# Half-height projections and one bank for the turned scores in a four-head expert attention

## What is computed

```python
sx = einsum('bsh,ndh->bnsd', x, hl_w) + hl_b        # 4 heads n, d = 16
q = einsum('bnsd,neod->bneso', sx, wq)              # 4 expert queries e per head
k = einsum('bnsd,nod->bnso', sx, wk)
v = einsum('bnsd,nod->bnso', sx, wv)
scores = einsum('bnesd,bntd->bnest', q, k) * d ** 0.5 + causal
att = softmax(scores, axis=-1)
qkv = einsum('bnest,bntd->bnesd', att, v)
# then a gate over e, the mix, two layer norms and a small feed-forward network
```

## Time and profile before

| | |
|---|---|
| median of 3 runs | 2512.23 us (2507.62 to 2513.51) |
| profiled execution | 2496.42 us |
| its span | 2494.4 us |
| TensorE busy over the span | 77% |
| VectorE busy over the span | 69% |
| ScalarE busy over the span | 37% |

### The profile page before, as it was taken

How to read it: one execution, slowest core, us unless ns; L and a number is a source line. 1 busy time by engine, 2 the same in 40 slices (tenths; PEclk the granted TensorE clock), 3 DMA queues, 4 the chain that set the end, 5 groups by cost and what they waited for, 6 DMA issues and landing times. The chain is left out here.

```text
span 2494.4 us, 51482 instructions
## 1 busy us (share of the span) xinstructions
PE 1922.1 (77%) x15831; PEld 1495.5 (60%) x15831; DVE 1715.0 (69%) x5200; ACT 919.3 (37%) x2958; POOL 1029.3 (41%) x878
## 2 busy tenths in 40 slices
PE   6888888799999999999999626777533332999970
PEld 2367767677777777777777414556422221887860
DVE  0069888358888888888888659999588883333223
ACT  2354343234444444444444238888422210111100
POOL 0023332013434434434443322222168875777772
PEclk9966676589999999999999656777755555555555
DMA  9900000000000000000000000000000002655526
GB/s 297 320 10 0 0 0 0 1 2 2 2 1 0 0 0 0 0 0 0 0 0 0 1 0 1 1 1 0 1 19 23 22 23 83 183 165 150 156 85 160
DMA packets 119880, 106.65 MB, mean 43 GB/s; under 512 B 62448, under 2 KB 109680, under 8 KB 118896
## 3 DMA queue, kind: packets, MB, share of 16 engines
q1 hardware_dynamic: 87024, 73.88, 11.0%
q10 hardware_dynamic: 18432, 16.79, 2.3%
q0 software_dynamic: 14336, 14.91, 1.8%
HBM read 78.84 MB, written 26.67 MB: 42 GB/s over the span
## 5 line engine op out<-in xcount | busy, mean ns | idle before, releaser
L988 ACT ACTIVATE arena<-PS 128x384 f32<-128x384 f32 (+3 forms) x384 | 178.3, 482 | 562.2 <-DMA arena<-in_t_experts_dram 216.5
L1336 POOL DMA_INDIRECT expert_rows<-arena x256 | 246.9, 965 | 104.4 <-issue 77.6
L1494 DVE TENSOR_REDUCE XR<-PS 128x2 f32<-128x192 f32 (+2 forms) x768 | 173.7, 280 | 107.4 <-PE PS L642 107.2
L642 PE MATMUL PS<-arena 32*128 32x96 f32 (+2 forms) x3072 | 235.0, 286 | 0.0
L1323 POOL DMA_INDIRECT routed_rows<-XR,SLu x192 | 199.8, 1041 | 74.9 <-issue 68.2
L642 PEld LDWEIGHTS PS<-arena 32*128 32x128 f32 x3072 | 199.1, 193 | 20.7
L1024 ACT ACTIVATE XR<-PS 128x256 f32<-128x256 f32 x512 | 167.3, 381 | 67.2 <-PE PS L657 67.0
L1277 POOL TENSOR_TENSOR arena<-arena,mhalf 96x16 f32<-96x16 f32 x32 | 92.7, 2896 | 225.8 <-DVE arena L1540 225.8
L1498 DVE TENSOR_TENSOR XR<-PS,XR 128x192 f32<-128x192 f32 (+2 forms) x768 | 172.4, 278 | 0.0
L609 PE MATMUL PS<-arena,WP 128*128 128x192 f32 x640 | 152.1, 363 | 18.4 <-ACT arena L988 17.8
L657 PE MATMUL PS<-WP,XR 128*128 128x128 f32 (+1 forms) x1024 | 163.7, 284 | 1.0 <-ACT XR L1024 1.0
(11 more groups left out here) (304 smaller groups left out, 4716.9 us busy)
## 6 DMA issues: line engine op xcount, KB each, us to landing
arena<-in_x_dram SPq DMA_DIRECT2D x32, 784.0 KB, 9.2
arena<-in_t_experts_dram ACTq DMA_DIRECT2D x128, 128.0 KB
arena<-in_t_experts_dram SPq DMA_DIRECT2D x128, 128.0 KB
routed_rows<-zt SPq DMA_DIRECT2D x16, 528.0 KB, 6.2
arena<-routed_rows SPq DMA_DIRECT2D x64, 132.0 KB
expert_rows<-arena POOLq DMA_INDIRECT x256
WP<-in_t_pack_dram SPq DMA_DIRECT2D x1, 3425.0 KB, 19.4
routed_rows<-XR,SLu POOLq DMA_INDIRECT x192, 2.2
```

The lines of the kernel that those rows point to most:

```text
L642: mm = pe.matmul(PS[:, i, S_AT[j]:S_AT[j] + QB * (j + 1)], qF[rows, u, 3 * b + j, :], kF[rows, u, keys], start=False, stop=True, skip_grou ...
L988: return act.activation(dst, src, ACT.Identity, **kw)
L1336: pool.indirect_dma_start(YD, bass.IndirectOffsetOnAxis(yi[:, u % 4, k:k + 1], 0), yb[:, u % 4, k, :], None).then_inc(e_st[u % 2], 16)
L1494: dve.tensor_reduce(negmax[:, p, j, :], PS[:, 0:2, S_AT[j]:S_AT[j] + QB * (j + 1)], AX_X, ALU.max, negate=True).then_inc(b_max, 1)
```

## The change

Keys and queries: each of the two matmuls of `project` takes only the 64 rows in which its images lie, and writes a bank of its own (`Q_` and `Q_ + 1`, now banks 2 and 3). The result comes out ordered by row half and not by image, so the consumers read it at `at = 2 * (b % 2) + b // 2`, and ScalarE's copies read two banks of 192 columns in one instruction. Turned scores: both heads of a turn go into one bank (`T0_`, now bank 6), ScalarE takes the exponential of 512 columns in one instruction, and `b_exp` counts once per turn. The transposes of the next turn wait for the whole exponential of the last one.

```diff
-            T0_, O_, F_, Q_, Z_ = 2, 4, 5, 6, 7
+            Q_, O_, F_, T0_, Z_ = 2, 4, 5, 6, 7
...
-                    o = PS[:, bk, 0:G * NTOK].rearrange("p (q r t) -> p q r t", q=2, r=2)[:, :, par, :]
-                    mm = pe.matmul(o, w[:, par, :], sxF[:, u, :].rearrange("p (q t) -> p q t", q=2),
+                    mm = pe.matmul(PS[:, Q_ + par, 0:FC], w[halves(par), par, :], sxF[halves(par), u, :],
                                    start=True, stop=True)
...
+                    at = 2 * (b % 2) + b // 2
...
-                        keys = slice(b * NTOK, b * NTOK + QB * (j + 1))
+                        keys = slice(at * NTOK, at * NTOK + QB * (j + 1))
...
-                            if n == 0:
-                                wait(pe, b_exp, 2 * k - 1 + i)
-                            mm = pe.transpose(PS[0:keys, T0_ + i, n * P:(n + 1) * P], Pe[:, p, i, n * P:n * P + keys], ident[:, :])
+                            if n == 0 and i == 0:
+                                wait(pe, b_exp, k)
+                            mm = pe.transpose(PS[0:keys, T0_, (2 * i + n) * P:(2 * i + n + 1) * P], Pe[:, p, i, n * P:n * P + keys], ident[:, :])
...
-                    pe.wait_ge(b_exp, (g * G + b) * 4 + 4)
+                    pe.wait_ge(b_exp, (g * G + b) * 2 + 2)
...
-                act.activation(kF[:, u, :], bank(Q_, P, G * NTOK), ACT.Identity,
+                act.activation(kF[:, u, :].rearrange("p (r n) -> p r n", r=2), PS[:, Q_:Q_ + 2, 0:FC], ACT.Identity,
...
-                    for i in range(2):
-                        act.wait_ge(b_pt, ((g * G + b) * 2 + p) * 2 + i + 1)
-                        act.activation(PT[:, b % 2, 2 * p + i, :], bank(T0_ + i, P, 2 * P), ACT.Exp).then_inc(b_exp, 1)
+                    act.wait_ge(b_pt, ((g * G + b) * 2 + p) * 2 + 2)
+                    act.activation(PT[:, b % 2, 2 * p:2 * p + 2, :].rearrange("p h n -> p (h n)"), bank(T0_, P, 4 * P),
+                                   ACT.Exp).then_inc(b_exp, 1)
```

More of the change, by code:

```diff
@@ L603, in b_values, with project @@
                 to_tokens(sxF[:, u, :], F_, GC).then_inc(b_vs, 1)
-            def project(w, u, bk):
+            def project(w, u):
                 for par in range(2):
-                    o = PS[:, bk, 0:G * NTOK].rearrange("p (q r t) -> p q r t", q=2, r=2)[:, :, par, :]
-                    mm = pe.matmul(o, w[:, par, :], sxF[:, u, :].rearrange("p (q t) -> p q t", q=2),
+                    mm = pe.matmul(PS[:, Q_ + par, 0:FC], w[halves(par), par, :], sxF[halves(par), u, :],
                                    start=True, stop=True)
@@ L615, in b_keys @@
                 wait(pe, b_gd, g - 2)
-                project(f_wk, u, Q_).then_inc(b_k, 1)
+                project(f_wk, u).then_inc(b_k, 1)
             def b_query(e):
@@ L621, in stage @@
                     wait(pe, b_qk, g * NE + e)
-                    project(f_wq[:, :, e, :], u, Q_).then_inc(b_q, 1)
+                    project(f_wq[:, :, e, :], u).then_inc(b_q, 1)
                 return stage
@@ L638, in stage @@
                     for j in BANDS:
-                        keys = slice(b * NTOK, b * NTOK + QB * (j + 1))
+                        keys = slice(at * NTOK, at * NTOK + QB * (j + 1))
                         for i in range(2):
                             rows = slice(32 * (2 * p + i), 32 * (2 * p + i) + 32)
-                            mm = pe.matmul(PS[:, i, S_AT[j]:S_AT[j] + QB * (j + 1)], qF[rows, u, 3 * b + j, :],
+                            mm = pe.matmul(PS[:, i, S_AT[j]:S_AT[j] + QB * (j + 1)], qF[rows, u, 3 * at + j, :],
                                            kF[rows, u, keys], start=False, stop=True, skip_group_check=True)
@@ L1013, in stage @@
                     wait(act, b_s, (g - 1) * 2 * G)
-                    copy_out(qF[:, u, :, e * QB:(e + 1) * QB],
-                             bank(Q_, P, G * NTOK).rearrange("p (m t) -> p m t", t=QB)).then_inc(b_qk, 1)
+                    copy_out(qF[:, u, :, e * QB:(e + 1) * QB].rearrange("p (r m) t -> p r m t", r=2),
+                             PS[:, Q_:Q_ + 2, 0:FC].rearrange("p r (m t) -> p r m t", t=QB)).then_inc(b_qk, 1)
                 return stage
@@ L1439, in _ @@
             dve.wait_ge(a_h, NG)
-            dve.memset(PS[64:P, 2:4, P:2 * P], 0.0).then_inc(b_clear, 1)
-            O_, F_, Q_, Z_ = 4, 5, 6, 7
+            dve.memset(PS[64:P, 6, :].rearrange("p (i n c) -> p i n c", i=2, n=2)[:, :, 1, :], 0.0).then_inc(b_clear, 1)
+            Q_, O_, F_, Z_ = 2, 4, 5, 7
             def groups_of(t, n):
```

## The result

The changed kernel is slower: median 2614.65 us (2611.74 to 2630.39) against 2509.93 us for the kernel before in the same comparison, ratio 1.043, 95% interval 1.039 to 1.048. The profiled execution has a span of 2609.8 us against 2494.4, 115 us more. Forecast were 2500 us and a chance of 0.08 for slower.

The account below looks back on a forecast made before the run. A ring of waits between engines, not TensorE alone, bounds the attention stage; 10.5 us from two projections plus 2 us at the start, 12.5 together, take 2512.2 to 2500 us, range 2486 to 2511 us.

Parts of the forecast that it names:

- The ring: Attention turn's cycle of waits between engines, 28.85 us; only `b_query(1)` and `b_query(2)` of five projections lie on it.
- the 10.5 of the sum: Attention stage: two projections on the cycle save 0.35 us a turn, over 30 turns at full clock 10.5 us.
- The 2 us for the first groups: First two groups, at 0.70 of full clock: TensorE sets the pace with all five projections, estimated 2 us saved.
- The cost of a projection: One `project` call on TensorE, start to start: 0.75 us before, 0.52 us at 64 rows.
- step costs: TensorE changing tile height: stepping out priced at 0.09 us, slower start of the piece behind at 0.06 us.
- Keys, `b_query(0)` and `b_query(3)` "at nothing": These three projections gain nothing in steady turns, because VectorE's chain covers them; without that cover, 0.34 us a turn.
- The rival: Granted clock falls around the grown idle time before `b_query(1)`; 2527 us with one turn at the lower level; chance 0.07.
- the growth to 0.9 us: TensorE's wait before `b_query(1)` grows from 0.53 to about 0.9 us as keys and `b_query(0)` shrink.
- Its price of 27 us: A whole attention turn at the 1.2 GHz level would last some 27 us longer.
- The chain behind 1016.05 "as long as now": VectorE's stretch from 1016.05 until L1513 ends at 1029.30, busy without a sizeable wait, keeps its length.
- The turned scores and the two-bank copies: Single 512-column exponential and ScalarE's copies from two banks: taken as no gain and no cost.

Follow-up runs that it names:

- b4: Changed kernel with keys and first query projection at 128 rows, and GpSimd's fourth-image pad-mask multiply moved before the power: 2501.81 us, ratio 0.999.
- c3: Changed kernel with only second and third query projections at 64 rows, other three at 128, GpSimd's pad-mask multiply moved before the power: 2605.61 us, ratio 0.998.
- b2: Changed kernel with only keys and the first query projection over 64 rows, the other three over 128: 2541.57 us, ratio 1.015.
- c1: Changed kernel, all five projections over 64 rows, with GpSimd's fourth-image pad-mask multiply moved before the power: 2665.38 us, ratio 1.019.
- c4: Kernel before, GpSimd's pad-mask multiply not mentioned as moved, with one of the last query projection's two matmuls left out: 2619.12 us, ratio 1.004.
- b1: Changed kernel with keys and the first query projection over 128 rows, the other three over 64: 2517.42 us, ratio 1.007.
- a1: Kernel before with the turned-scores half of the change alone; projections stay over 128 rows into one bank: 2505.15 us, ratio 0.999.
- a2: Changed kernel with every projection over all 128 rows again, still into two banks and in the new image order: 2505.88 us, ratio 1.000.
- b3: Changed kernel with the half-height matmul pairs of keys and the first query issued twice, the other three once: 2520.87 us, ratio 1.009.
- a4: Kernel before with one of the two full-height matmuls of every projection left out: 2543.84 us, ratio 1.012.
- a3: Changed kernel with every half-height pair of matmuls issued twice: 2525.39 us, ratio 1.010.
- c2: Kernel before with only GpSimd's fourth-image pad-mask multiply moved before the power: 2610.42 us, ratio 1.000.

## Why the prediction was wrong

- **The ring** held. Two of five projections count: 13.44 us against 13.76 for their part of the turn, and b4 and c3 have the turn of 28.5 us. Full use of the change at full clock would have been some 30 x 0.32 = 10 us, the 10.5 of the sum. The 2 us for the first groups no run shows: the first L731 comes at 568 us before and at 561 to 579 in the others, without a pattern.
- **The cost of a projection** held: 0.53 us for 0.52, and step costs of the size taken. The Trainium skill's table in "TensorEngine Tiling (Array Packing)", section Overview, says up to 2x, which taken in full is an estimate of 0.37 us saved. Measured are 0.75 - 0.53 = 0.22, before the slower start of the piece behind, so the trace stays well within that "up to".
- **Keys, `b_query(0)` and `b_query(3)` "at nothing"** is the step that failed. I priced work taken from TensorE beside the ring at nothing, because another engine's chain covers it. It isn't free: in keys and the first query it turns into waiting of TensorE (0.53 to 0.90 us before the second query), and around this wait the granted clock falls to the lower level. b2 has only these two at half height and is 1.5% slower; c1, where this place alone is left, is 1.9% slower. `b_query(3)` at half height did no such thing: with the multiply moved, L676 waits as long with it (b4, c1) as without (c3). A whole matmul less there does (c4, 0.4% slower).
- **The rival was there, its chance and size were wrong.** I named the place before the second query and the growth to 0.9 us, and gave it 0.07 because no window of the stage came near a fall. That was no evidence: the windows of the earlier trace rows show a clock of 1.00 whether the margin is large or small. I let one turn at the lower level stand for the whole rival. Its price of 27 us was not far off: a turn has 890 / 78 x 28.8 = 329 records, which at the 290 in 43 us of the dip take 49 us, so 20 us more, an estimate. But there were many dips, and the records of 800 us price them at 118 us. The second place, L676, I didn't name.
- **The chain behind 1016.05 "as long as now"** failed too. L1457 grew by 0.26 us beside GpSimd's multiply and gave back most of 0.32. b4 and c1 show this by moving the multiply: turn 28.53 us with it moved, 28.78 to 28.80 without. It cost twice, since the late VectorE is also what lifted L676's wait to 0.34 us and opened the second place for the clock: moving the multiply took away both (b1 to b4, changed kernel to c1), and brought the changed kernel's loss from 4.3 to 1.9%.
- **The turned scores and the two-bank copies** at nothing: right (a1, a2).

What stays open: why a wait of 0.34 us in one place does what 0.53 us in another doesn't. The two lie in different surroundings, and no run varied those. At L676 the wait was changed without touching a matmul. Before the second query it was only ever changed by the work just ahead of it, so there the longer wait and the lighter work are not told apart. Open as well are why one turn in five falls and not each, and why the changed kernel's dips are so long. It was not tried whether filling TensorE's waits in c3 would remove the dips at the stage's two ends.

## What to carry to other kernels

Where TensorE is busy nearly all of the time and isn't on the ring that sets the pace, work taken from it can become waiting, and in this kernel the granted clock fell around such waits and slowed everything: take work only from the pieces on the ring, and leave, or put back, the rest. Before such a change, list each wait of TensorE in a turn and how much each grows; a clock of 1.00 in the profile says nothing of the margin. A gain of a few tenths of a microsecond on one engine shifts it against its neighbours: look for which instruction then runs beside what.

## What was not expected of the hardware

- The granted clock fell to its lower level in a stage where TensorE was busy 97% of the time, behind single waits of 0.34 us (b1, b3, c4) and inside or just behind waits of 0.9 us (b2, c1). Not each such wait brought a fall. In the changed kernel one such stretch lasted 44 us, though TensorE was busy without a pause in it (43.00 of 43.00 us).
- Removing work slows: a4, with a third of a microsecond less in each of five places, is 1.2% slower than before; a3, with work done twice, keeps the clock.
- A VectorE instruction over 96x4 elements takes 0.17 us alone. Where it starts inside a GpSimd multiply over 96x256, it ends 0.02 to 0.03 us behind that multiply, wherever it began: 0.43 us when started 0.32 us into it (changed kernel), 0.69 us when started 0.05 us into it (a4). It is held, not slowed. Inside GpSimd's power over 96x16 it keeps its 0.17 us (b4).
- The kernel before took 2505 us on one chip and 2612 us on another. The attention stage was not the cause: a turn of a1 on the first took 28.86 us, of c2 on the other 28.84. The difference lies behind 1850 us, where 644 us remain in the kernel before and 750 in c2.
